# Two up tiles share their low-rank products, and the third tile of a unit starts one job earlier

## The reference, cut to what matters

```python
def dequant_nf4(codes, absmax, shape):
    vals = NF4[codes] * jnp.repeat(absmax, BLOCK)
    return vals.reshape(shape)
w_up = dequant_nf4(w_up_codes, w_up_absmax, (H, D)).T          # D = 1024, H = 2752
y1 = x1 @ w_up + b_up + x1 @ w_up_lora_a @ w_up_lora_b          # rank R = 16
x2 = jax.nn.relu(y1)
w_down = dequant_nf4(w_down_codes, w_down_absmax, (D, H)).T
y2 = x2 @ w_down + b_down + x2 @ w_down_lora_a @ w_down_lora_b
...
x = x + _L0_ffn_ref(_L0_cond_ref(x, ...), ...)
x = x + _L1_ffn_ref(_L1_cond_ref(x, ...), ...)
```

## Time and profile before

| what | value |
|---|---|
| runs shown | 1476.39, 1479.58, 1480.91 us; median 1479.58 |
| the profiled execution | 1473.9 us, of which the span 1472.4 us |
| the loops of jobs | about from 110 to 1000 us of the span |
| granted TensorE clock, mean over the span | 0.982 |
| VectorE busy, ScalarE busy | 76%, 52% of the span |

### The profile page before, as it was taken

One profiled execution on the slowest core, in us unless ns is written; L12 is line 12 of the kernel. 1 busy time (PEld: TensorE's weight loads), 2 busy tenths in 40 slices (PEclk: granted clock), 3 DMA queues, 4 the chain that ended last, 5 costly groups with the idle time before them and its releaser, 6 DMA issues.

```text
span 1472.4 us, 20741 instructions
## 1 busy us (share of the span) xinstructions
PE 1413.0 (96%) x6815; PEld 1159.7 (79%) x6815; DVE 1125.5 (76%) x1075; ACT 761.7 (52%) x845; POOL 197.3 (13%) x214
## 2 busy tenths in 40 slices
PE   7999999999999999999999999999999499999996
PEld 7887888888888888888888888888755388888775
DVE  6868788778778787877787878874234599999884
ACT  5554644545545446445455454461113177777762
POOL 0110000000000000000000000000001234475643
PEclk9999999999999999999999999999999699999998
DMA  6854647568566676566675676764558455959951
GB/s 212 312 218 156 226 188 275 201 237 282 198 257 235 210 283 223 211 263 213 252 252 204 243 255 225 266 235 165 206 186 313 150 156 155 343 169 325 324 149 30
DMA packets 104339, 331.40 MB, mean 225 GB/s; under 512 B 17204, under 2 KB 24892, under 8 KB 104220
## 3 DMA queue, kind: packets, MB, share of 16 engines
q1 hardware_dynamic: 81492, 258.56, 47.0%
q0 software_dynamic: 22512, 71.32, 17.0%
q10 hardware_dynamic: 256, 0.40, 0.1%
HBM read 295.10 MB, written 46.14 MB: 232 GB/s over the span
## 4 chain that ended last, share of the span: by engine, by line
PE 91%; DVE 4%; issue 2%; ACT 1%; DMA 1%; ACTq 0%; SPq 0%; POOL 0%; DVEq 0%; POOLq 0%
PE pair L1087 27%; PE pair L1089 26%; PE pair L1088 26%; PE pair L1139 4%; PE pair L1231 2%; DVE wf L791 2%; PE pair L1298 1%; PE pair L1149 1%; PE pair L1239 1%; PE pair L1152 1%; PE pair L1247 1%; PE pair L1135 1%; PE pair L1123 1%; DMA z_rows<-z 0%; DMA xcv<-x_conv 0%
## 5 line engine op out<-in xcount | busy, mean ns | idle before, releaser
L791 DVE TENSOR_TENSOR wf<-wf,term 128x1024 f32<-128x1024 f32 x308 | 377.1, 1224 | 91.7 <-ACT term L587 72.1
L587 ACT ACTIVATE term<-codes 128x1024 f32<-128x1024 int32 x308 | 321.1, 1055 | 109.5 <-DVE wf L791 109.4
L1087 PE MATMUL pair<-wh,hh 128*128 128x512 f32 x704 | 276.7, 393 | 4.0 <-DVE acc L830 2.6
L1089 PE MATMUL pair<-wh,hl 128*128 128x512 f32 x704 | 275.4, 391 | 0.0
L1088 PE MATMUL pair<-wl,hh 128*128 128x512 f32 x704 | 275.3, 391 | 0.0
L1087 PE MATMUL pair<-ring,wh 128*128 128x512 f32 x656 | 255.8, 390 | 0.7 <-issue 0.6
L1089 PE MATMUL pair<-ring,wl 128*128 128x512 f32 x656 | 255.3, 389 | 0.0
L1088 PE MATMUL pair<-ring,wh 128*128 128x512 f32 x656 | 255.2, 389 | 0.0
L836 DVE TENSOR_TENSOR acc<-acc,pair 128x1024 f32<-128x1024 f32 x160 | 194.7, 1217 | 66.4 <-PE pair L1089 66.3
L724 ACT ACTIVATE whr<-wraw 128x1024 fp32r x184 | 188.1, 1055 | 90.5 <-PE pair L1089 54.6
L1062 DVE TENSOR_TENSOR wlr<-wraw,whr 128x1024 fp32r<-128x1024 f32 x184 | 213.4, 1216 | 13.1 <-ACT whr L724 12.8
(11 more groups left out here) (166 smaller groups left out, 1469.9 us busy)
## 6 DMA issues: line engine op xcount, KB each, us to landing
ring<-x_parts SPq DMA_DIRECT2D x320, 512.0 KB, 7.0
wraw<-exp_w SPq DMA_DIRECT2D x64, 512.0 KB
x_parts<-stage POOLq DMA_DIRECT2D x24, 512.0 KB, 6.0
xg<-exp_b POOLq DMA_DIRECT2D x23, 512.0 KB, 8.0
codes<-codes_up SPq DMA_DIRECT2D x22, 512.0 KB, 6.9
codes<-codes_dn SPq DMA_DIRECT2D x22, 512.0 KB, 6.7
am<-am_dn SPq DMA_DIRECT2D x22, 512.0 KB, 3.8
acc<-x_nat POOLq DMA_DIRECT2D x16, 512.0 KB, 5.1
```

Of the source, the lines that this page charges most:

```text
L587: return nc.scalar.activation(out, codes[:, n % 2], ACT.Relu, scale=scale, bias=-scale * bend)
L791: nc.vector.tensor_tensor(whole(n), whole(n), term[:, e % 2], op).then_inc(term_added, 1)
L1087: mm(ps, ah, bh, start=first, stop=False)
L1089: return mm(ps, al, bh, start=False, stop=last)
```

## The change

For every unit but the first (tiles n of 4 and more), the two up tiles' low-rank products are made together. A matmul has the same 128-column piece of the table as weights, and both slots of `lora_t` (256 columns) as the moving operand; 8 such matmuls make what 16 made. They run in two halves of 4: the first in `down` of the second job, the second in `up` of the third job, after its second K tile. VectorE adds each half to half of both tiles (`add_half`), so both tiles are finished in the third job, where `high` and `low` of both now stand. The third tile (the first down tile) has its `head` and first two ramps at the end of the second job on ScalarE, and their additions there on VectorE.

```diff
             def lora_high(i, n):
                 act.wait_ge(lora_in, i * 128 + 16 * (n + 1))
-                wait(act, ab_mm, i * 8 + n - 1)
+                wait(act, ab_mm, i * 8 + n - (n % 4 != 2))
...
             def high(i, n):
-                act.wait_ge(w_ready, i * 8 + n + 1)
+                act.wait_ge(w_ready, i * 8 + n + 1 + (n >= 4 and n % 4 == 0))
...
-                    if not early:
+                    if not early and k % 4 in (0, 3):
                         high(i, k + 3)
                     lora_high(i, k + 4)
-                    head(i, k + 4)
-                    ramps(i, k + 4, range(1, 7))
+                    if k % 4 == 2:
+                        ramps(i, k + 4, (3, 4))
+                        high(i, k + 2)
+                        high(i, k + 3)
+                        ramps(i, k + 4, (5, 6))
+                    else:
+                        head(i, k + 4)
+                        ramps(i, k + 4, range(1, 7))
...
                     ramps(i, k + 4, (7,))
+                    if k % 4 == 1:
+                        head(i, k + 5)
+                        ramps(i, k + 5, (1, 2))
...
             def add_lora(i, n):
+                if n >= 4 and n % 4 < 2:
+                    if n % 4 == 1:
+                        add_half(i, n, 0)
+                    return
...
+            def add_half(i, n, h):
+                dve.wait_ge(ab_mm, i * 8 + n + h)
+                dve.wait_ge(scaled, i * 8 + n + 1)
+                both = wf[:, n // 4 % 2, 0:2, h * 512:(h + 1) * 512].rearrange("p s (c n) -> p s c n", n=P)
+                nc.vector.tensor_tensor(both, both, pair[1][:].rearrange("p (c s n) -> p s c n", c=4, n=P),
+                                        ALU.add).then_inc(w_ready, 1)
...
+                        else:
+                            add_ramps(i, k + 4, (3,))
+                            add_half(i, k + 3, 1)
+                            add_ramps(i, k + 4, (4,))
+                            low(i, k + 2)
+                            add_ramps(i, k + 4, (5,))
+                            low(i, k + 3)
+                            add_ramps(i, k + 4, (6,))
...
                     add_lora(i, k + 4)
+                    if k % 4 == 1:
+                        add_ramps(i, k + 5, (1,))
                     add_down(i, k, 3)
+                    if k % 4 == 1:
+                        add_ramps(i, k + 5, (2,))
...
+            def lora_pair(i, n, h):
+                if h == 0:
+                    pe.wait_ge(lora_ready, i * 8 + n + 1)
+                wait(pe, w_ready, i * 8 + n - 1 + h)
+                for c in range(4):
+                    ins = mm(pair[1][:, c * 2 * P:(c + 1) * 2 * P], lora[:, (4 * h + c) * P:(4 * h + c + 1) * P],
+                             lora_t[:].rearrange("p s n -> p (s n)"), start=True, stop=True)
+                ins.then_inc(ab_mm, 1)
...
             def lora_product(i, n):
+                if n >= 4 and n % 4 < 2:
+                    if n % 4 == 1:
+                        lora_pair(i, n, 0)
+                    return
...
-                        up(i, k + 1).then_inc(up_mm, 1)
+                        up(i, k + 1, halves=(i, k + 3) if k % 4 == 2 else None).then_inc(up_mm, 1)
                     down(i, k, (i, k + 4))
```

More of the change, by code:

```diff
@@ L903, in _ @@
                     else:
-                        add_ramps(i, k + 4, (1,))
-                        low(i, k + 3)
+                        if k % 4 != 2:
+                            add_ramps(i, k + 4, (1,))
+                        if k % 4 in (0, 3):
+                            low(i, k + 3)
                         lora_low(i, k + 4)
-                        add_ramps(i, k + 4, range(2, 7))
+                        if k % 4 != 2:
+                            add_ramps(i, k + 4, range(2, 7))
+                        else:
[4 more added lines that the diff above has]
+                            add_ramps(i, k + 4, (5,))
+                            low(i, k + 3)
+                            add_ramps(i, k + 4, (6,))
                         hidden_low(i, k + 1)
@@ L1153, in lora_product, with up @@
                 ins.then_inc(ab_mm, 1)
-            def up(i, q, between=None):
+            def up(i, q, between=None, halves=None):
                 pe.wait_ge(wl_ready, i * 8 + 4 * (q // 4) + 2)
@@ L1174, in up @@
                         lora_product(*between)
+                    if kt == 1 and halves:
+                        lora_pair(*halves, 1)
                 return ins
```

## The result

| | kernel before | changed kernel |
|---|---|---|
| first timing | 1477.99 us median of 4 (1471.65 to 1480.91) | 1458.70 us median of 4 (1455.95 to 1464.15), ratio 0.988, 95% interval 0.9834 to 0.9926 |
| timed again, more runs | 1474.98 us median of 30 (1465.05 to 1482.83) | 1460.49 us median of 7 (1452.03 to 1465.95), ratio 0.9911, interval 0.988 to 0.9942 |
| profiled execution, span | 1472.4 us | 1455.4 us |

The change makes the kernel faster, by about 1%: 13 us by the second ratio, with an interval from 9 to 18.

What follows compares the result with a forecast made beforehand. TensorE, busy 96% of the span, was taken to bound the kernel; 8.2 us from ten units plus 2.8 from the first pass made 11.0, so 1479.6 - 11.0 = 1468.6 us, range 1465.0 to 1475.0.

Steps and rivals of the forecast that it cites:

- the base of 1479.6: Median in us of the runs shown of the kernel before, from which the predicted saving was subtracted.
- the 11.0: Whole kernel: predicted saving in us, 8.2 from ten units plus 2.8 from the first pass.
- The price of a wide matmul: TensorE's low-rank products: a 256-column matmul estimated at 0.12 us, with bounds 0.105 and 0.210.
- the 0.05: Matmul behind an up tile's product takes 0.28 us instead of 0.23; this extra was predicted to go.
- The rival that columns set the price: A 256-column matmul costs 0.210 us, twice a 128-column one; 3.8 us saved in all, 1475.8; chance 0.07.
- The unit's 0.82: Us saved per unit of four jobs: low-rank half-products cost 0.97 instead of 1.79.
- 90.0 us instead of 90.9: Sign of being right: time of four jobs, with TensorE busy for all of it.
- The cover in the third job: VectorE and ScalarE still deliver in time: `hidden_low` start 610.6 with VectorE 0.2 before, `add_down` 1.1 us spare.
- the rival with the dear one: Strided half-addition costs d above 1.21 us; at 3.6 us the kernel is 19 us slower, 1498; chance 0.08.
- The "2.8 us" for the stall: First pass, second job: TensorE's 2.56 us wait for `add_down` at 141.42 and 0.28 slow start both go.
- the cover of the first job: With the product behind step 1 gone, 0.6 us of its cover is left; nothing on VectorE or ScalarE moves later.
- the 2 and 1.3 us allowed for spread: Run spread in the range's ends: some 2 us below 12.2 faster (1465.0), 1.3 above first pass at 0.146 (1474.7).

Runs made afterwards that it cites:

- the narrow kernel: Changed kernel with each 256-column product issued as two 128-column matmuls, order kept: 1471.29 us median of 11, ratio to before 0.9981.

## Where the prediction failed, and what it had right

The mechanism was read rightly and the time wrongly: 1458.7 us against 1468.6. The step that failed is the last of the sum, the base of 1479.6 from which the 11.0 was taken and the spread allowed around it; it is worked out at the end of this section, behind the terms.

**What bounds the kernel** was read rightly: in settled jobs a microsecond of TensorE is one of the kernel, and 0.87 less per unit came through whole.

**The price of a wide matmul** was the choice among ends from 0.105 to 0.210, and 0.12 is what was measured. The reading behind it holds too: the narrow kernel pays 0.84 + 0.05 whatever the order, its matmuls follow their weight loads, and the 0.05 is gone behind a wide block. The rival that columns set the price is out. The rule of the Trainium skill (TensorE: Matmul & The Clock Gate, "Back-to-back issue gap", 56 ns at 128 columns and 109 at 256, estimates) is out too, with 105 and 120 measured; the section itself gives it for an isolated matmul and says that it counts too little for short ones with their weight loads. The unit's 0.82 came as 0.87, 0.5 us too little over ten units; 0.83 are in the blocks themselves (2 x 0.895 less 2 x 0.48), and 0.04 were not traced further. The sign "90.0 us instead of 90.9" was added up wrongly: the four jobs of the earlier trace rows make 89.95, so by the prediction's own 0.82 it had to be 89.1, and 89.08 was measured.

**The cover in the third job** came as laid out. Timeline of VectorE there (start, us):

```profile
591.00 0.28 DVE L832 TENSOR_TENSOR lora_t<-lora_raw,lora_t 32x128 fp32r<-32x128 f32 x1 [0.51 <-ACT lora_t L612]
591.95 1.23 DVE L802 TENSOR_TENSOR wf<-wf,term 128x1024 f32<-128x1024 f32 x1 [0.67 <-ACT term L587]
593.09 1.22 DVE L827 TENSOR_TENSOR wf<-wf,pair 128x1024 f32<-128x1024 f32 x1
...
597.33 1.23 DVE L802 TENSOR_TENSOR wf<-wf,term 128x1024 f32<-128x1024 f32 x1 [0.67 <-ACT term L587]
598.47 1.22 DVE L837 TENSOR_TENSOR wl<-wf,wh 128x1024 fp32r<-128x1024 f32 x1
599.60 1.22 DVE L802 TENSOR_TENSOR wf<-wf,term 128x1024 f32<-128x1024 f32 x1
601.27 1.23 DVE L842 TENSOR_TENSOR hl<-pair,hh 128x1024 fp32r<-128x1024 f32 x1 [0.45 <-ACT hh L627]
```

9.4 us on, these are the prediction's ramp 3 at 601.4, half-addition at 602.5, ramp 5 at 606.9, second `low` at 608.0, ramp 6 at 609.2 and `hidden_low` at 610.6, each within 0.2 us. VectorE is there 0.45 early where 0.2 was forecast. A half-addition takes 1.22 us, so the rival with the dear one is out. (In that rival a half-addition of 2.7 us is where the whole kernel would be slower; a unit is longer than before already from about 2.5, by its own 2d - 0.5 less 1.3 against 0.82.)

**The first pass** was priced too high by most profiles and too low by two. The "2.8 us" for the stall came as 2.0: 53.88 less 51.05, without the unit's 0.87. Of the missing 0.8, 0.7 is a new wait: the prediction counted the cover of the first job in settled jobs (0.6 left) and not in this pass, whose first job lost the product behind step 1 and has another order on VectorE. TensorE now waits there 0.43 us for the `add_down`, and its matmul is 0.27 slow to start:

```profile
116.71 0.50 PE L1124 MATMUL pair<-wh,hh 128*128 128x512 f32 x1 [0.43 <-DVE acc L852]
```

Against that, the old wait comes with a low clock in two of five profiles, at 1.7 and 2.7 us; the sum took its price from a profile in which that didn't happen.

**What had no term** is the turns of the passes. Their row was quoted, "issue: 0.6" in the earlier trace rows, and passed over. They cost 0.7 to 1.5 us in four profiles of the kernel before and nothing now. With them the change gives, first pass and later ones together, 11.8 to 12.1 us in profiles without a fall of the clock, and 14.1 in the one with it. That the 11.0 of the sum comes so near is in part luck: the units gave 0.5 more than it says, the turns 1.2 that it doesn't have, and the first pass 0.8 less.

**The step that failed** is the last: "the loss is the same in each, so 1479.6 - 11.0". Its base, the median of three runs, stood 4.6 us above that of the thirty runs taken later, and the 2 and 1.3 us allowed for spread were far too little for times between 1465 and 1483. From 1475.0 the sum of 11.0 leads to 1464.0, and with the 12.7 that the terms above make on average (8.7 of the units, 1.2 of the turns, 2.8 of the first pass with its clock) to 1462.3. So of the 9.9 us 4.6 are the base and 1.7 the terms. The other 3.6 are not traced to anything; they lie within the spread of the runs, as does the 1460.5 of seven runs (1452 to 1466). The 1.8 and 3.1 us ahead of the loops and behind them in the first pair of profiles are not the change: they came out otherwise in the other profiles (start 106.6 to 110.6, end 470.4 to 477.6).

Not tried: a version with the second `add_down` of the first job earlier, for the 0.7 us that its new wait costs; by the times alone it couldn't be told from the changed kernel. No kernel of the study has shorter loops than the changed one.

## What to carry to other kernels

Compare what a matmul costs at two widths in the trace before cutting columns or instructions: here a quarter of the columns cost half the time because weight loads set the pace of the short matmuls, and joining two products under one set of weights was worth nearly one of them (0.83 of 0.895 us). A product that serves two consumers comes later for the first, so reckon the whole chain of the engines behind it; here the order of two engines off the path decided between 13 us gained and 55 lost. And take the spread of the time from many runs before giving a range: here runs of one kernel lay up to 18 us apart, more than the gain, and marks inside the loops, repeatable to 0.02 us in the changed kernel, told what the total could not.

## What the runs showed of the chip that was not expected

A matmul of 128 columns with the same weights as the one before it is no cheaper: eight take 0.84 us, weights new each time or every second time, and each has its own weight load in the trace. The turn of a loop can cost TensorE up to 0.93 us where the loop is fetched anew in every pass (57 instead of 30 packets of instruction fetches), and 16 small matmuls ahead of the loop switch that on. A wait of 2.5 us costs 1.7 or 2.7 us more in two executions of five, because the granted clock is at its lower level for some us behind it; after waits of 4.9 us the one shown above was followed by a clock of 0.50 for 2.7 us.
